# Query stacks through memory, key and query parts in stack order, and one 448-column matmul more per group of scores

## The reference, cut to what matters

```python
x = x + tanh(g_xattn[0]) * L0_xattn(ctx_1024, layernorm(x))    # a time-warping alignment
x = x + tanh(g_ffn[0])   * L0_ffn(layernorm(x))                # 256 -> 1024, conv, silu, -> 256
x = x + tanh(g_xattn[1]) * L1_xattn(layernorm(x), ctx_1024)    # 16 heads, 112 queries, 375 keys
x = x + tanh(g_ffn[1])   * L1_ffn(layernorm(x))                # top-k pattern network

# L1_xattn, for each of the 8 batches and 16 heads of width 16
scores = einsum('bhqd,bhkd->bhqk', q * 16 ** -0.5, k)
out = einsum('bhqk,bhkd->bhqd', softmax(scores), v) @ Wo.T + bo
```

## Time and profile before

| | |
|---|---|
| runs shown | 644.6, 645.31, 645.93 us; median 645.31 |
| the profiled execution | 645.01 us, its span 643.3 us |
| mean granted clock of TensorE | 0.782 |
| busy PE, PEld, DVE, ACT, POOL | 428.2, 306.5, 430.2, 273.0, 99.4 us |
| DMA | 45,770 packets, 47.16 MB |

### The profile page before, as it was taken

How to read it: one execution, slowest core, us unless ns; L and a number is a source line. 1 busy time by engine, 2 the same in 40 slices (tenths; PEclk the granted TensorE clock), 3 DMA queues, 4 the chain that set the end, 5 groups by cost and what they waited for, 6 DMA issues and landing times.

```text
span 643.3 us, 10182 instructions
## 1 busy us (share of the span) xinstructions
PE 428.2 (67%) x3448; PEld 306.5 (48%) x3448; DVE 430.2 (67%) x1714; ACT 273.0 (42%) x635; POOL 99.4 (15%) x201
## 2 busy tenths in 40 slices
PE   2998799622392403657989888899999655406306
PEld 2667685511272103635767666677455553106303
DVE  4645999799736896868776676775454665473573
ACT  4744544812303861024455454665533452351340
POOL 7900000000052561335800000000000000000000
PEclk9998699755585855667798898999999887855556
DMA  4560004292006992002699794700300361000001
GB/s 133 153 162 1 2 1 154 65 207 77 2 1 107 136 135 24 1 1 60 158 128 176 118 218 52 72 2 1 121 11 2 119 218 56 2 0 1 1 1 58
DMA packets 45770, 47.16 MB, mean 73 GB/s; under 512 B 5198, under 2 KB 43927, under 8 KB 44695
## 3 DMA queue, kind: packets, MB, share of 16 engines
q1 hardware_dynamic: 45718, 46.51, 35.3%
HBM read 37.80 MB, written 8.60 MB: 72 GB/s over the span
## 4 chain that ended last, share of the span: by engine, by line
PE 54%; DVE 25%; ACT 9%; issue 6%; SPq 3%; DMA 2%; POOL 0%; DVEq 0%; ACTq 0%
PE ps L1959 7%; PE ps L1913 4%; PE ps L1900 4%; PE ps L1889 4%; DVE PR L980 4%; ACT below L1594 4%; PE ps L1735 4%; PE ps L1743 3%; PE ps L1875 3%; SPq L548 3%; PE ps L1799 3%; PE ps L2085 2%; DMA ctxP<-in_ctx 2%; DVE prod L976 2%; PE ps L1694 2%
## 5 line engine op out<-in xcount | busy, mean ns | idle before, releaser
L1141 DVE TENSOR_REDUCE negm<-ps 112x1 f32<-112x375 f32 x128 | 66.3, 544 | 21.5 <-PE ps L1889 18.4
L1565 ACT ACTIVATE E<-ps 125x448 f32<-125x448 f32 x96 | 52.1, 543 | 57.0 <-PE ps L1900 56.8
L1889 PE MATMUL ps<-ks,qs 96*112 96x375 bf16 x128 | 46.6, 378 | 13.6 <-issue 10.2
L2058 PE MATMUL ps<-cnt,same 128*128 128x3 bf16 (+4 forms) x40 | 6.9, 173 | 61.8 <-ACT below L1594 43.4
L1913 PE MATMUL ps<-E,v 125*32 125x112 f32 x768 | 42.9, 275 | 0.0
L1900 PE MATMUL ps<-qs,ks 99*125 99x112 bf16 x384 | 41.0, 232 | 0.9 <-ACT E L1565 0.5
L1900 PEld LDWEIGHTS ps<-qs,ks 99*125 99x125 bf16 x384 | 35.3, 144 | 10.0 <-issue 6.7
L1129 DVE TENSOR_REDUCE acts<-gel 128x4 f32<-128x448 f32 x32 | 19.8, 620 | 29.3 <-ACT gel L1528 29.3
L2058 PEld LDWEIGHTS ps<-cnt,same 128*128 128x128 bf16 (+1 forms) x40 | 4.4, 110 | 65.1 <-issue 65.1
L727 POOL CAST kp<-kx 128x750 bf16<-128x750 f32 x8 | 6.5, 811 | 168.7 <-ACT path L1477 143.0
L1889 PEld LDWEIGHTS ps<-ks,qs 96*112 96x112 bf16 x128 | 17.7, 142 | 25.3 <-issue 19.4
(11 more groups left out here) (363 smaller groups left out, 1129.9 us busy)
## 6 DMA issues: line engine op xcount, KB each, us to landing
ks<-key_parts SPq DMA_DIRECT2D x48, 187.5 KB, 8.5
piw<-fn_process_input_weights SPq DMA_DIRECT2D x8, 1024.0 KB, 4.9
key_parts<-kp SPq DMA_DIRECT2D x16, 281.2 KB, 4.7
ctx_again<-in_ctx SPq DMA_DIRECT2D x7, 512.0 KB
ctxP<-in_ctx SPq DMA_DIRECT2D x8, 375.0 KB
keys<-kx SPq DMA_DIRECT2D x16, 187.5 KB, 2.2
kx<-keys SPq DMA_DIRECT2D x8, 375.0 KB, 6.6
patn<-in_L_ffn_input_patterns SPq DMA_DIRECT2D x1, 2048.0 KB, 17.8
```

Source lines behind the costliest of these rows:

```text
L1141: drain(dve.tensor_reduce(negm[:, n:n + 1], bank(nm)[0:S, 0:SC], AX.X, ALU.max, negate=True), nm)
L1565: drain(fn(E[:, (KCH * f + c) % 6, :], bank(nm)[0:KC, 0:4 * S], ACT.Exp), nm)
L1889: fill(mm(bank(nm)[0:S, 0:SC], qs[0:SR, u // 4 % 3, n, :], ks[0:SR, u // 4 % 3, n, :], start=True, stop=True), nm)
```

## The change

Five edits, as one diff:

1. The parts of keys lie in HBM as (16 features, 16 heads, 375) in place of (256, 375), so that a row of a stack is one run of 12,000 bytes. A batch is stored by six DMAs in place of two.
2. Only the first batch's query stacks (u < 4) are still made by PE. For the others the query parts are stored to HBM (`query_parts`, 2 x 6 DMAs) and loaded as stacks, one set of six DMAs for batches 0 to 3 (`load_queries(0)`), one for 4 to 7 (`load_queries(1)`).
3. SP's and POOL's lists are put in another order: `split_keys(3)` stands before the FFN's adds; parts 3 are stored before the attention; `load_stack(3)` and `load_queries(1)` stand between the stores of parts 5 and 6; `patn`, `oiwn`, `opat` and `pval` come one or two stacks later.
4. The maxima of a group are transposed by one matmul of 112 columns into 12 rows, copied by ACT in place of DVE, against 12 rows with ones in three of them for each head (`kones`). `smax` works in pairs of banks: two matmuls, one reduction over both.
5. Before the four score matmuls of c = 0, one matmul of 448 columns writes the same bank; its result is overwritten.

```diff
-                    sp.dma_start(ks[HD * j:HD * j + HD, b % 3, :, :],
-                                 key_parts[b, part].rearrange("(n d) s -> d n s", d=HD)
-                                 ).then_inc(stack_loaded[b % 3], 16)
+                    sp.dma_start(ks[HD * j:HD * j + HD, b % 3, :, :], key_parts[b, part]).then_inc(stack_loaded[b % 3], 16)
...
                 for t in range(2):
-                    sp.dma_start(key_parts[b, :, 128 * t:128 * t + 128, :].rearrange("c p s -> p c s"),
-                                 kp[:, b % 2, t, :, :]).then_inc(parts_stored[b % 2], 16)
+                    for c in range(3):
+                        sp.dma_start(key_parts[b, c, :, 8 * t:8 * t + 8, :].rearrange("d n s -> n d s"),
+                                     kp[:, b % 2, t, c, :]).then_inc(parts_stored[b % 2], 16)
...
-            for b in range(3):
+            for b in range(4):
                 store_parts(b)
                 load_keys(b + 2)
-                load_stack(b)
-            for b in range(3, B):
+                if b < 3:
+                    load_stack(b)
+            def store_queries(half):
+                for t in range(2):
+                    sp.wait_ge(q_split, 2 * half + t + 1)
+                    for c in range(3):
+                        sp.dma_start(query_parts[half, c, :, 8 * t:8 * t + 8, :].rearrange("d n s -> n d s"),
+                                     qp[:, t, c, 448 * half:448 * half + 448]).then_inc(queries_stored[half], 16)
+            def load_queries(half):
+                sp.wait_ge(queries_stored[half], 96)
+                lo = S if half == 0 else 0
+                for j, part in enumerate(Q_PARTS):
+                    sp.dma_start(qs[half][HD * j:HD * j + HD, :, lo:HB * S], query_parts[half, part, :, :, lo:HB * S]
+                                 ).then_inc(loaded[f"q{half}"], 16)
+            store_queries(0)
+            load_queries(0)
+            store_queries(1)
+            for b in range(4, B):
                 store_parts(b)
                 if b + 2 < B:
                     load_keys(b + 2)
-            for b in range(3, B):
+                if b == 5:
+                    wait_filled(sp, ("scoreT", 3, KCH - 1))
+                    load_stack(3)
+                    sp.wait_ge(queries_stored[0], 96)
+                    wait_filled(sp, ("qstack", 3))
+                    load_queries(1)
+            for b in range(4, B):
                 wait_filled(sp, ("scoreT", 4 * b - 9, KCH - 1))
                 load_stack(b)
...
             wait_drained(pool, ("path", 0))
-            for b in range(3):
+            for b in range(4):
                 split_keys(b)
             for c in range(HT):
...
-                    wait_drained(pe, ("qstack", u))
+                    if u < 4:
+                        wait_drained(pe, ("qstack", u))
+                    if u == 4:
+                        pe.wait_ge(loaded["q0"], 16 * len(Q_PARTS))
+                    if u == 4 * HB:
+                        pe.wait_ge(loaded["q1"], 16 * len(Q_PARTS))
...
+                for e in range(2):
+                    n = 4 * (u % 4) + 2 * i + e
+                    ins = mm(psum[0:S, 2 * i + e, 0:SC], queries_of(u, n)[0:SR], ks[0:SR, u // 4 % 3, n, :],
+                             start=True, stop=True)
+                fill(ins, nm)
+            def queries_dense(f):
+                return ks[0:SR, f // 4 % 3, 0:2, :].rearrange("p n s -> p (n s)")[:, 0:448]
...
+                if c == 0:
+                    mm(bank(nm)[0:KC, 0:448], ks[0:SR, f // 4 % 3, 0, 0:KC], queries_dense(f), start=True, stop=True)
...
-                for i in range(4):
-                    ins = mm(bank(nm)[SR:SR + 3, S * i:S * i + S], negp[:, f // 4 % 2, 4 * (f % 4) + i, :],
-                             identb[0:S, 0:S], start=True, stop=True)
-                fill(ins, nm)
+                n = 4 * (f % 4)
+                fill(mm(bank(nm)[SR:SR + MR, 0:S], negp[:, f // 4 % 2, n:n + 4, :].rearrange("p n c -> p (n c)"),
+                        identb[0:S, 0:S], start=True, stop=True), nm)
```

More of the change, by code:

```diff
@@ L27 @@
 SR = HD * len(K_PARTS)
+MR = 4 * 3
 LAG = 5
@@ L149, in plan_psum @@
     for f in range(-LAG - 1, 4 * B + 4):
-        if 0 <= f + LAG + 1 < 4 * B:
-            p.add(("qstack", f + LAG + 1), 3)
+        if 0 <= f + LAG + 1 < 4:
+            p.add(("qstack", f + LAG + 1), 4 + (f + LAG + 1) % 2)
         if 0 <= f + LAG < 4 * B:
-            for i in range(4):
-                p.add(("smax", f + LAG, i), (4 * (f + LAG) + i) % 3)
+            for i in range(2):
+                p.add(("smax", f + LAG, i), 2 * i, 2 * i + 1)
         if 0 <= f < 4 * B:
@@ L206, in build_program @@
                   wq_in, bq_in, wk_in, bk_in, wv_in, bv_in, wo_in, bo_in,
-                  pat_in, piw_in, pval_in, oiw_in, opat_in, out, key_parts, keys):
+                  pat_in, piw_in, pval_in, oiw_in, opat_in, out, key_parts, keys, query_parts):
     plan = plan_psum()
@@ L330, in build_program @@
         meet = [rd.take(f"meet{d}", [128, KB, 128]) for d in range(2)]
+        kones = Region(rd.at - 2 * 4 * KB * 128).take("kones", [MR, 4, SC], BF16)
         scratch = Region(rw.at + 4 * CT * B * D)
@@ L478, in bankb @@
             return ps[plan[name].banks[0]][:, :].bitcast(BF16)
-        names = ("x",) + tuple(f"ctx{b}" for b in range(B)) + ("again", "ones_k", "attnW", "ffnW", "small", "biasT", "pat", "oiw",
+        names = ("x",) + tuple(f"ctx{b}" for b in range(B)) + ("again", "ones_k", "q0", "q1", "attnW", "ffnW", "small", "biasT", "pat", "oiw",
                  "opat", "pval", "piw0", "piw1")
@@ L494, in build_program @@
              "pmx_ready pmd_ready pexp_ready vec scl pol").split()]
+        queries_stored = [sem(f"queries_stored{i}") for i in range(2)]
+        kones_ready = sem("kones_ready")
         parts_stored = [sem(f"parts_stored{i}") for i in range(2)]
@@ L648, in _ @@
                 did(pool.memset(t[:, :], 0.0))
-            for t in (ones, same[0], same[1], onesb):
+            for t in (ones, same[0], same[1]):
                 did(pool.memset(t[:, :], 1.0))
@@ L713, in _ @@
             pool.memset(warm[:, :], 0.0).then_inc(meet_ready, 1)
+            wait_filled(pool, "joinF")
+            wait_filled(pool, "joinG")
+            did(pool.memset(kones[:, :, :], 1.0))
+            settle()
+            did(pool.affine_select(out=kones[:, :, :], in_=kones[:, :, :], compare_op=ALU.is_ge, fill=0.0, base=0,
+                                   pattern=[[-3, 4], [0, SC]], channel_multiplier=1))
+            settle()
+            pool.affine_select(out=kones[:, :, :], in_=kones[:, :, :], compare_op=ALU.is_ge, fill=0.0, base=2,
+                               pattern=[[3, 4], [0, SC]], channel_multiplier=-1).then_inc(kones_ready, 1)
             for k in range(2):
@@ L1183, in _ @@
                 if u < 4 * B and u % 4 == 3:
-                    for i in range(3):
-                        wait_drained(dve, ("smax", u, i + 1))
+                    for i in range(2):
+                        wait_drained(dve, ("smax", u, i))
                     part = negp[:, u // 4 % 2, :, :]
```

84 lines of the change are left out of this document (40 added, 44 removed).

## The result

The changed kernel takes 654.17 us (median of 4 runs, 650.57 to 659.11), the kernel before in the same job 645.62 (644.6 to 647.45): a ratio of 1.0142 with a 95% interval of 1.0099 to 1.0186. It is slower, as forecast, but by 9 us and not by 25. The profiled execution took 652.47 us.

A forecast was written before the change was run, and what follows sets the result against it. The loop from stack to stack was taken to set the pace, not the sum of PE's work. 645.0 + 14.2 (FFN) + 0 (start) + 10.6 (stack 4) + 0.9 (periods) = 670.7, said as 670 us; range 650 to 682.

The forecast's parts named there:

- FFN: POOL's first convolution add waits behind `split_keys(3)` for keys 3: +10.2, and +4 for the fuller queue, +14.2 us.
- start: Start of the attention: first real scores +2.5 us, four groups give back about 2.6, so 0 (ends -2 to +3).
- stack 4: Stack 4 queues behind `load_queries(1)` and the stores of parts 6 and 7: its `smax` +10.6 us (+8.5 to +13).
- the three periods after it: Batch periods after batch 4's first `smax`: 19.1 us each against 18.8, +0.9 us in all.
- last groups and what follows: End of the attention: the last groups save three times 0.55 us and have a colder start: 0.
- Wide rows: Edit 1, key stack loads: the rate stays with 12,000-byte packets, as 16 partitions are still written; 14 us a stack.
- The other end that I wrote: Key stack at the 128-partition rate: 3.4 + 2.9 = 6.3 us.
- the signs that I named: Stacks near 100 GB/s, POOL waiting until near 227, stalls of about 15 us before batch 4 and 4 before others, then half clock.
- The rival that expected overlap: "Only POOL's queue counts": `load_queries(1)` and stack 4 overlap, stack 4 is in time, 660 us; chance 0.13.
- four lighter groups: First attention groups, with fewer query matmuls: -0.55 us each at full clock, -1 at half, about 2.6 back.
- The loop: Attention, stack to stack: less work only lengthens the stall to 4 us; 5.3 for 5.6 after it; extra matmul 0.

The follow-up runs named there:

- the version with both orders: Changed kernel with `split_keys(3)` behind POOL's FFN adds and `load_queries(1)` before stack 3 on SP's queue: 638.87 us, ratio 0.9883 (median of all ten runs 641.87).
- the kernel with most of it, 89 us: Changed kernel without edit 1 (two stores a batch, stacks loaded in rows of 750 bytes): 667.98 us, ratio 1.0354.

## Why the forecast was right in direction and wrong in size

The terms of the sum, from the first `smax` of each batch. The measured ones add up to the change of the span, 650.4 - 643.3 = 7.1.

| step | forecast | measured |
|---|---|---|
| FFN, to the first `smax` of all | +14.2 | +13.8 (293.5 to 307.3) |
| start, to the first `smax` of batch 3 | 0 | +2.2 (+16.0 less 13.8) |
| stack 4 | +10.6 | +5.0 (24.7 less 19.7) |
| the three periods after it | +0.9 | -10.4 (46.0 less 56.4) |
| last groups and what follows | 0 | -3.5 |

- **The step that failed is "Wide rows": "By the rows the rate stays ... I take 14 us".** It takes 10.9. The inference compared a 3-, a 16- and a 128-partition load, of which the first two have equal packets, and concluded that packet size plays no part; the rows showed that width matters, not that length doesn't. 14 to 10.9 is worth 3 us a period, so most of the -10.4 in the three periods. The rest is the group behind the stand, 5.3 us in the sum and 3.6 in two of the three (395.26 and 409.81 to the next request): PE stood only 1 us there, not 4, and the clock stayed whole. The run without edit 1 (668) is 14 us longer, of the missing 16, but not all of it is this term: 9.1 us are in the three periods, and the others in the start and the last groups, with 41 us more of half clock. The other end that I wrote, 6.3 us, was reached by no set of 16-partition loads. Of the signs that I named, POOL's wait came (its add at 226.6, I had said near 227), and the stalls were 5.9 us before batch 4 and 1 before the next two, not 15 and 4.
- **Stack 4.** The queueing behind `load_queries(1)` is there (with the queries asked for first the period is 16.1), but its pieces had other sizes. By the sizes of the packets stack 3's data flow from 341 to 349 us (8 us, 11.3 forecast), the queries' from 349 to 360 (11, 13.5 forecast), the stores' of parts 6 and 7 from 360 to 370 (5.5 forecast) and stack 4's from 366 to 376, in part beside them: the loads were sized too long and the stores too short. SP itself was held too: issuing the twelve stores took it 18.2 us, and so it asked for stack 4 at 365.0, some 7 us after the last scores of batch 1 (358). The rival that expected overlap was right in a small part: the transfers are still mostly one behind the other.
- **FFN.** Right in place and cause: POOL waits for keys 3, +13.2 at the add. The size came out partly by luck, for two misses nearly cancel: SP asks for keys 3 6.2 us later, where I had counted 4 in all, and they land 3.2 us sooner after that. Not seen was that undoing it alone gives back 2 us and not 13; the profile shows 17 us more of half clock with the earlier start. Terms don't simply add up here.
- **Start.** The wait for `q0` came, but its data landed at 320.9, which is 307.1 without the FFN's 13.8: 3.4 us sooner than forecast. The first real scores are at 323.9 against 309.3, +0.8 beyond the FFN (forecast +2.5). The 2.6 us that four lighter groups were to give back did not come: they ran at 5.0 us a group. I had priced the half clock after a stall, and not that a wait of 6 us in this place comes with a long stretch of it.
- **The loop** stayed the bound with a smaller period, and the extra matmul hid where it was said to. The tail gave 3.5 where I had 0: 0.8 until the attention ends (448.2 to 458.0 is +9.8) and 2.7 behind it, in a part that the change does not touch, where the stretches at half clock add up to 7 us less.

Not settled is what keeps a busy PE at half clock for 20 to 44 us in some places, while after waits of 5.5 to 9 us in others the clock is back within 3 to 6. Nor why the profiles with 37 us of it are not slower than those with 34.

## What to carry to other kernels

A chain set by one transfer is worth measuring by that transfer alone, with row length, width and target varied one at a time, before an edit of its layout is priced: here 3 us in 14 decided the size of the result. Look at every new wait of PE for what the clock does in the groups behind it; filling the one here gave a whole clock there, but no gain of time that could be told. And issue the transfers on one queue in the order of need: the same change is +1.4% with two pieces of work out of order and about -1% with both put right.

## What the hardware showed that I had not expected

- Loads into 16 partitions: rows of 750 bytes 12.9 to 13.5 us for 1.152 MB, of 768 bytes 11.8 for 1.180 MB, of 672 bytes 11.0 for 1.032 MB, of 12,000 bytes 10.8 for 1.152 MB; into one group of partitions 12.2 in place of 10.7; three loads of 32 partitions 7.1, one of 96 6.8.
- A store whose outer length is 8 takes 1.8 times as long as one of 128 (4.97 against 2.79 us of data). By the rule of the Trainium skill ("DMA: Bandwidth & Descriptors", Why a DMA increments its semaphore by 16 and not by 1), the largest number up to 16 that divides the outer lengths of both sides, it has 8 engines in place of 16, which would be twice the time by my estimate; the 1.8 of the packets comes near.
- TensorE at 1.2 GHz for 30 to 44 us while its rows are busy: a group with PE busy in 5.01 of 5.01 us stays at 0.50. In the changed kernel the clock fell within a wait of 6.4 us, in the version with both orders within one of 6.7; 34 matmuls in that wait removed it there. Waits of 7.7 and 9.0 us elsewhere brought 6.9 and 10.2 us of it.
- Kernels repeat very differently: 10 runs of the one with the queries first spread over 22 us (641.7 to 663.7), all runs of the kernel before in every job over 13 (639.7 to 652.8). The half clock alone does not explain it: the kernel with most of it, 89 us, spread over 7 (664.1 to 671.4, 6 runs).
